# Attention's TensorE order: in three half steps of each window, the natural scores move ahead of a turn and the transposed scores

## The reference, cut to what matters

```python
B, D, L = 16, 128, 512                     # x and ctx_2048: (16, 128, 512)
qh = layernorm(x).reshape(B, 8, 16, 512)   # 8 heads of depth 16
kh = vh = ctx_2048.reshape(B, 8, 16, 512)
qk = einsum('bhdq,bhdl->bhql', qh, kh) * 16 ** -0.5
ret = einsum('bhql,bhdl->bhdq', softmax(qk, axis=-1), vh)
x = x + tanh(g_xattn[0]) * gamma * ret.reshape(B, 128, 512)
x = x + tanh(g_ffn[0]) * ffn(layernorm(x))  # mixture of 8 experts, top 2, a shared expert, a core path
```

## Time and profile before

| | us |
|---|---|
| median of 3 runs (lowest, highest) | 737.02 (733.06, 739.28) |
| span of the profiled execution, first to last instruction | 740.6 |
| attention, 16 windows of natural scores | about 13.5 to 348 |
| one window in the steady stretch | 20.7 |
| busy share over the span: PE, DVE, ACT, POOL | 93%, 71%, 73%, 65% |

### The profile page before, as it was taken

The page is one execution under the profiler, slowest core; times in us unless marked ns, Lnnn a source line. Parts: engine busy times, 40 slices in busy tenths (PEclk is TensorE's granted clock), DMA queues, the critical chain, the costliest instruction groups (busy, mean ns, idle before and its releaser), DMA issues.

```text
span 740.6 us, 20875 instructions
## 1 busy us (share of the span) xinstructions
PE 687.7 (93%) x6101; PEld 373.9 (50%) x6101; DVE 526.1 (71%) x855; ACT 541.0 (73%) x1129; POOL 479.4 (65%) x474
## 2 busy tenths in 40 slices
PE   1799988999999999999999889799999999999998
PEld 0122222323333333223355444488888888888844
DVE  4999998999999999998887746534444444444456
ACT  2399988999999999999895656376666767676511
POOL 3558788888888888986477142135666656566732
PEclk9999999999999999999999989999999999999999
DMA  6555666566665666545355634489987888887487
GB/s 209 190 157 189 197 195 205 176 201 219 205 193 192 207 208 216 176 139 181 97 170 176 208 117 145 155 169 168 142 123 116 122 121 120 101 109 98 57 268 259
DMA packets 136993, 123.98 MB, mean 167 GB/s; under 512 B 70612, under 2 KB 106452, under 8 KB 136920
## 3 DMA queue, kind: packets, MB, share of 16 engines
q1 hardware_dynamic: 122056, 106.58, 50.7%
q0 software_dynamic: 13632, 15.47, 14.9%
q10 hardware_dynamic: 1232, 0.98, 0.4%
HBM read 60.33 MB, written 51.53 MB: 151 GB/s over the span
## 4 chain that ended last, share of the span: by engine, by line
PE 72%; DVE 9%; DMA 6%; issue 5%; ACT 3%; POOL 2%; SPq 1%; another core or an unknown queue 1%; ACTq 0%; DVEq 0%; POOLq 0%
PE EH L1309 24%; PE Y L1309 16%; PE pv L562 13%; PE ring L549 9%; DVE mx L708 6%; PE nat L537 5%; ACT P L633 2%; DMA k_scratch<-khl 1%; PE ring L581 1%; DVE statx L689 1%; POOL y_sums L2136 1%; PE ring L572 1%; SPq L396 1%; DMA rd<-den_scratch 1%
## 5 line engine op out<-in xcount | busy, mean ns | idle before, releaser
L708 DVE TENSOR_REDUCE mx<-nat 128x2 f32<-128x1024 f32 x256 | 296.7, 1214 | 24.0 <-PE nat L537 23.1
L633 ACT ACTIVATE P<-ring 128x512 f32<-128x512 f32 x512 | 279.4, 603 | 20.4 <-PE ring L549 10.5
L2136 POOL DMA_INDIRECT y_sums<-ysb,to x84 | 138.2, 1645 | 100.5 <-DVE ysb L2070 86.7
L562 PE MATMUL pv<-P,VT 128*32 128x256 f32 x2048 | 159.0, 395 | 0.4
L537 PE MATMUL nat<-KS,QS 48*128 48x512 f16 x512 | 111.7, 397 | 25.7 <-DMA QS<-q_scratch 15.6
L549 PE MATMUL ring<-QS,KS 49*128 49x512 f16 x512 | 123.5, 392 | 8.4 <-ACT P L633 8.4
L1673 ACT ACTIVATE X<-EH,bcur 128x256 f32<-128x256 f32 x168 | 85.6, 560 | 50.5 <-DVE u L2024 26.0
L1309 PE MATMUL Y<-whi,u 128*128 x672 | 117.1, 273 | 0.3 <-DVE u L2024 0.3
L1309 PE MATMUL EH<-XA,whi 128*128 128x256 f16 x672 | 116.9, 273 | 0.3 <-DMA XA<-g_rows 0.3
L2024 DVE TENSOR_TENSOR u<-X,u 128x512 f16<-128x512 f32 x84 | 57.8, 688 | 77.1 <-ACT u L1679 76.4
L1309 PE MATMUL EH<-XA,wlo 128*128 128x256 f16 x336 | 91.6, 273 | 0.0
(11 more groups left out here) (267 smaller groups left out, 985.1 us busy)
## 6 DMA issues: line engine op xcount, KB each, us to landing
XA<-in_wall SPq DMA_DIRECT2D x8, 800.0 KB, 4.4
u<-in_wall SPq DMA_DIRECT2D x8, 800.0 KB, 4.4
QS<-q_scratch SPq DMA_DIRECT2D x64, 96.0 KB, 2.6
KS<-k_scratch SPq DMA_DIRECT2D x62, 96.0 KB, 2.3
X<-in_x SPq DMA_DIRECT2D x16, 256.0 KB, 2.9
q_scratch<-qhl SPq DMA_DIRECT2D x16, 256.0 KB, 2.1
xr<-in_x SPq DMA_DIRECT2D x16, 256.0 KB, 3.6
rd<-den_scratch SPq DMA_DIRECT2D x16, 256.0 KB
```

The lines of the kernel that those rows point to most:

```text
L562: m = pe.matmul(pv[32 * j:32 * j + 32, q], VT[i][:, lb, g, j, :], Pb[4 * (s % 2) + j][:, q], start=(lb == 0 and half == 0), stop=(lb == 3) ...
L633: act.activation(Pb[4 * (s % 2) + j][:, :], bank[:, :], ACT.Exp).then_inc(t_use.sem, 1)
L708: dve.tensor_reduce(mx[:, k // 8, :, k % 8], nat[k % 2][:, :, :], AX.X, ALU.max).then_inc(t_max.sem, 1)
L2136: pool.indirect_dma_start(out=ysum[:, :], out_offset=bass.IndirectOffsetOnAxis(ap=to[:, j % 2, a:a + 1], axis=0), in_=ysb[j % 2][:, a, :], ...
```

## The change

The turn of maxima that stood at the end of step 0 (group 1 of element w - 1), the turn of values that stood at the end of step 1, and the turn of maxima that stood at the end of step 4 (group 0 of element w) now stand in the first half of the next step. In that half the order is: the natural scores, then the turn, then the two transposed scores, then the products. In all other halves the order is as before. In the list of `ring` entries nothing changes places, and the order of the instructions on ACT and on DVE is the same in both kernels.

```diff
             for half in range(2):
-                if 0 <= t < B:
-                    jobs += [("st", t, n, 2 * half), ("st", t, n, 2 * half + 1)]
-                if w < B:
-                    jobs.append(("nat", w, 2 * s + half))
+                scores = [("st", t, n, 2 * half), ("st", t, n, 2 * half + 1)] if 0 <= t < B else []
+                natural = [("nat", w, 2 * s + half)] if w < B else []
+                turns = []
+                if s == 1 and half == 0 and 1 <= w <= B:
+                    turns.append(("m", w - 1, 1))
+                if s == 2 and half == 0 and w < B:
+                    turns += [("vt", w, 0), ("vt", w, 1)]
+                if s == 5 and half == 0 and w < B:
+                    turns.append(("m", w, 0))
+                jobs += natural + turns + scores if turns else scores + natural
                 if 0 <= before < B and m % 4:
                     jobs.append(("pv", before, m, half))
                 elif 0 <= before < B and half:
                     jobs += [("pv", before, m, 0), ("pv", before, m, 1)]
-            if s == 0 and 1 <= w <= B:
-                jobs.append(("m", w - 1, 1))
-            if s == 1 and w < B:
-                jobs += [("vt", w, 0), ("vt", w, 1)]
-            if s == 4 and w < B:
-                jobs.append(("m", w, 0))
```

## The result

| | median us | lowest to highest | runs |
|---|---|---|---|
| before | 735.81 | 733.06 to 739.28 | 4 |
| changed | 743.93 | 741.93 to 744.90 | 4 |

The ratio is 1.0113, with a 95% interval of 1.0069 to 1.0157: slower by 5 to 12 us. The forecast was 743.0. The forecast was reckoned from a median of 737.0, that of three of the four runs before; from there the step is 6, measured it is 8.1. The profiled execution of the changed kernel took 741.93 us, 739.8 of them its span, so some 2.1 us lie around the span.

A forecast was written before the change was run, and what follows sets the result against it. PE's own path through three turns was taken to bound the window: 0.31 + 0.15 + 0.08 = 0.54, less 0.07 slack, gives +0.47 us in each of 13 windows, +6.1 on 737.0, so 743; range 731 to 749.

The forecast's parts named there:

- The bound: Attention windows: PE's own path through three turns to the next window's natural block 4 counts; there DVE only follows.
- the hole: DVE's idle 0.75 us per window at block 4; forecast to close and reopen at block 5 as 0.9 to 1.0.
- the hole closes: Rival: DVE bounds throughout, so 0.75 x 14 = 10.5 us would go, giving 726.5; chance 0.14, wholly or in good part.
- Step 5: Turn of group 0: natural scores go first, the turn and X0's exponent come later, X3 waits; +0.31 us per window.
- Step 1: Turn of group 1: X1's wait is covered, but X0's exponent ends later and delays X3; +0.15 us per window.
- Step 2: Turn of values: natural scores go ahead, the wait for ACT's copies behind the turn stays unfilled; +0.08 us per window.
- The slack of 0.07: Natural block 5 is done at 210.98, DVE reaches it at 211.05; these 0.07 us are subtracted from each window's loss.
- The exit price: Leaving a side-by-side pair for matmuls over all rows takes 0.31 us, some 0.09 more than staying among pairs.
- The sum: 0.31 + 0.15 + 0.08 less 0.07 gives +0.47 us per window; over 13 windows +6.1 us.
- the rows of maxima have time to spare: Rows sent 0.3 us later cost nothing, as the first transposed score needing one stands over 4 us behind.
- Dearer: Rival: following exponent pairs wait again, or each place costs 0.31 or more; +12 us, 749; chance 0.12.

The follow-up runs named there:

- only_c: Kernel before with only the turn of values (step 2) moved as in the change; mean window 20.78 us, ratio to before 1.0035 (1.0012 to 1.0058).
- only_a: Kernel before with only the turn of group 0 (step 5) moved as in the change; mean window 21.10 us, ratio to before 1.0065 (1.0041 to 1.0090).
- only_b: Kernel before with only the turn of group 1 (step 1) moved as in the change; mean window 20.84 us, ratio to before 1.0074 (1.0040 to 1.0108).
- fill_all: Kernel before with the order turn, natural, transposed scores at all three places; mean window 21.09 us, ratio to before 1.0028 (1.0001 to 1.0054).
- after_half_max: Changed kernel with each row maximum taken over the first 256 of 512 keys; mean window 21.27 us, ratio to before 1.0040 (1.0018 to 1.0063).
- fill_c: Kernel before with the order turn, natural, transposed scores at step 2 alone; mean window 20.56 us, ratio to before 0.9987 (0.9960 to 1.0014).

## Why the prediction was right

- **The bound.** That PE's path and not DVE sets the window was right: halving DVE's reductions gave 0.1 us per window and left the loss in place, and moving the natural scores ahead moved the hole from block 4 to block 5 (0.93, forecast 0.9 to 1.0). DVE isn't far behind, though: the window fell by 0.1 alone when DVE had half its work, because ACT's ring was next. The rival "the hole closes" is refuted by only_c, which made that move alone.
- **Step 5, +0.31.** Measured +0.32, in the changed kernel and in only_a. The mechanism, ACT idle ahead of the turn and X3 exactly on its wait, is shown by the halved exponents, which leave 0.10 for the exit and a remainder of 0.05.
- **Step 1, +0.15.** Measured +0.16 (2.06 to 2.22) and +0.15 in only_b; the wait of X1 went and one of X3 came.
- **Step 2, +0.08.** Measured +0.10; less slack, 0.08 in only_c.
- **The slack of 0.07.** It was 0.03: with the measured parts 0.32 + 0.16 + 0.10 - 0.03 = 0.55, and the window grew by 0.57 and not 0.47. I took the end of nat5 for the time at which DVE could start; DVE needs some 0.04 more (nat5 ends at 213.96, DVE starts at 214.00).
- **The exit price.** 0.31 was taken from natural scores to products; from natural scores to a turn it is 0.32.
- **The sum.** 13 x 0.57 would be 7.4, the forecast 6.1; attention takes 6.4 more in the traces, the medians differ by 8.1. That these lie so close is in part luck. The forecast put the windows that are still filling at nothing, and by the turn of values of the third window the changed kernel is already 3.7 us behind (62.97 against 59.30). The window from 100 us is 3.0 shorter (21.58 against 24.57), and the last ten windows together cost 4.9 (one of the ten is 0.66 longer than its neighbours in before). One trace of the changed kernel can't tell how much of the first two is the change and how much is scatter; they cancel for the most part. The windows of 0.57 are what is shown.
- **Wrong, without effect here:** that the rows of maxima have time to spare. The forecast gave them over 4 us; the row of group 0 has 3.99 before and 4.00 in the changed kernel, since what needs it moves along with the turn, and that is next to no time to spare: fill_all, after_half_max and one window of only_a paid for it.
- **"Dearer", 0.12:** its point, exponent pairs that each wait again, isn't seen; X3 waits once at each turn.

## What to carry to other kernels

A hole in a busy engine's row is worth closing only if the next thing it waits for isn't standing right behind; subtract the end of the following input from the time the engine would ask for it, before counting a gain. When work is moved ahead of something short that starts another engine's chain (a turn, a copy), the price is its own length plus what that chain then holds back; so look at what waits behind the starter. Where that is a wait with nothing in it, as behind the turn of values, independent work put there gains (fill_c, 0.14 per window). Where the starter's engine needs the next scores at once, as behind the turns of maxima, that work is in the way there too (fill_all, +0.22 and +0.06), and the old order was the best of the three tried. And when one limit is moved by a tenth of a microsecond per step, look for two or three others within the same tenth: here DVE, ACT's ring, the landing of the queries and the row of maxima all were.

## What the runs showed of the hardware

- Two matmuls on different halves of PE's rows give the way to another such pair after 0.22 to 0.23 us, and to a matmul over all rows after 0.31 to 0.32, whichever it is (products 0.31, turn of maxima 0.32, turn of values 0.32). One more exit of this kind at a place costs 0.10: with ACT and DVE out of the way from 1.32 to 1.42 us at the turn of group 0, and from 2.30 to 2.40 at the turn of values.
- The same program had medians of 736.3, 726.9 and 727.4 us in three series of runs, a difference of 1.3%, larger than most effects of this study. The first two series have the same chip number. Attention took the same time in both traces of this program (it ends at 348.4 and 348.0 us); as far as the traces show, the difference lies in the feed-forward part, and its cause is open.
- A row of maxima of 4 KB, sent by ACT's queue, can be read by PE some 4 us later or a little more: after 3.99 us without a wait in the kernel before, and after 4.08 to 4.53 us with a wait in five windows of fill_all and one of only_a (4.38).
